# Attention of a post-norm transformer layer: normalised in 32x32 blocks turned by VectorE, with new orders of all steps

## What is computed

```python
qkv = x @ Wqkv + bqkv                      # 16 heads of 16
scores = q @ k.T / 4 + alibi_causal_bias   # per head, -inf above the diagonal
out = softmax(scores) @ v                  # per head
x = layernorm(x + out @ Wo + bo)
wu, wg, wd = ternary_quant(W_up), ternary_quant(W_gate), ternary_quant(W_down)
x = layernorm(x + (silu(x @ wu.T) * (x @ wg.T)) @ wd.T)
```

## Time and profile before

| | |
|---|---|
| time, median of 3 runs | 621.96 us (621.37 to 624.52) |
| span of the profiled execution | 619.3 us (its own time is not listed beside the span) |
| PE busy | 583.6 us (94%) |
| DVE busy | 494.4 us (80%) |
| ACT busy | 318.8 us (51%) |
| POOL busy | 299.0 us (48%) |
| DMA | 68.49 MB, mean 111 GB/s |
| chain that ended last | PE 78%, DVE 5%, ACT 5%, POOL 5%, issue 4%, DMA 2% |

### The profile page before, as it was taken

How to read it: one execution, slowest core, us unless ns; L and a number is a source line. 1 busy time by engine, 2 the same in 40 slices (tenths; PEclk the granted TensorE clock), 3 DMA queues, 4 the chain that set the end, 5 groups by cost and what they waited for, 6 DMA issues and landing times.

```text
span 619.3 us, 12888 instructions
## 1 busy us (share of the span) xinstructions
PE 583.6 (94%) x4012; PEld 342.5 (55%) x4012; DVE 494.4 (80%) x1258; ACT 318.8 (51%) x593; POOL 299.0 (48%) x504
## 2 busy tenths in 40 slices
PE   5789888999999999999999999999999999999995
PEld 3344354664656555674556646575556646446674
DVE  5388968996799868989599877989599877993766
ACT  2129713459247644477246653476345753576262
POOL 1306695346275535465174543654264452654234
PEclk9789998999999999999999999999999999999998
DMA  6965715005462073502653064601644054600101
GB/s 158 289 175 206 211 51 161 23 29 163 122 172 66 3 229 115 166 1 83 161 166 100 1 199 123 160 28 52 186 144 127 1 166 105 206 2 3 35 1 35
DMA packets 47724, 68.49 MB, mean 111 GB/s; under 512 B 4857, under 2 KB 43641, under 8 KB 44793
## 3 DMA queue, kind: packets, MB, share of 16 engines
q1 hardware_dynamic: 47691, 68.08, 37.5%
HBM read 38.44 MB, written 29.36 MB: 109 GB/s over the span
## 4 chain that ended last, share of the span: by engine, by line
PE 78%; DVE 5%; ACT 5%; POOL 5%; issue 4%; DMA 2%; SPq 0%; POOLq 0%; DVEq 0%
PE ring L698 17%; PE max_bank L613 10%; PE acc L647 9%; PE ring L635 9%; PE ring L590 8%; PE acc L715 7%; PE ring L597 4%; ACT probs L772 4%; PE ring L671 4%; PE max_bank L618 2%; PE ring L655 2%; POOL probs L1042 2%; PE ring L684 1%; POOL tern_down L1085 1%; PE max_bank L715 1%
## 5 line engine op out<-in xcount | busy, mean ns | idle before, releaser
L772 ACT ACTIVATE probs<-ring 128x512 f32<-128x512 f32 x320 | 170.7, 606 | 45.6 <-PE ring L635 44.0
L1042 POOL TENSOR_SCALAR_AFFINE_SELECT probs<-probs 128x256 f32<-128x256 f32 (+1 forms) x320 | 120.5, 401 | 130.1 <-ACT probs L772 129.4
L896 DVE CUSTOM_DVE_ANT_0 max_bank<-max_bank,causal_wide 128x384 f32<-128x384 f32 (+1 forms) x256 | 157.2, 637 | 15.3 <-PE max_bank L613 12.2
L613 PE MATMUL max_bank<-k_stack,q_stack 112*128 112x384 bf16 (+3 forms) x512 | 123.4, 304 | 5.9 <-DVE neg_max L896 2.8
L1078 POOL TENSOR_TENSOR hidden_lo<-hidden,hidden_hi 128x512 f16<-128x512 f32 (+1 forms) x72 | 75.1, 1050 | 63.6 <-ACT hidden_hi L803 63.3
L635 PE MATMUL ring<-q_stack,k_stack 114*128 114x512 bf16 (+3 forms) x512 | 103.7, 300 | 1.6 <-DVE attn L921 0.5
L791 ACT ACTIVATE gating<-ring,tanh_scale 128x512 f32<-128x512 f32 (+1 forms) x72 | 45.8, 639 | 74.0 <-PE ring L698 74.0
L647 PE MATMUL acc<-probs,v_ones 128*32 128x512 f32 (+3 forms) x1024 | 79.9, 437 | 2.8 <-POOL probs L1042 2.8
L613 PEld LDWEIGHTS max_bank<-k_stack,q_stack 112*128 112x128 bf16 x512 | 46.5, 98 | 54.0 <-DVE neg_max L896 15.3
L900 DVE TENSOR_REDUCE neg_max<-max_bank 128x2 f32<-128x512 f32 (+1 forms) x96 | 63.7, 686 | 10.4 <-PE max_bank L618 8.7
L635 PEld LDWEIGHTS ring<-q_stack,k_stack 114*128 114x128 bf16 x512 | 44.5, 97 | 49.4 <-issue 17.0
(11 more groups left out here) (107 smaller groups left out, 866.0 us busy)
## 6 DMA issues: line engine op xcount, KB each, us to landing
q_stack<-qk_scratch SPq DMA_DIRECT2D x15, 768.0 KB, 6.1
k_stack<-k_slots SPq DMA_DIRECT2D x15, 768.0 KB, 7.8
qk_scratch<-qk_parts SPq DMA_DIRECT2D x16, 384.0 KB, 3.0
k_slots<-qk_parts SPq DMA_DIRECT2D x16, 384.0 KB, 2.6
xin<-x_dram SPq DMA_DIRECT2D x8, 512.0 KB, 3.5
qk_scratch<-qk_parts SPq DMA_DIRECT2D x16, 256.0 KB, 3.2
k_slots<-qk_parts SPq DMA_DIRECT2D x16, 256.0 KB, 2.3
res<-x_dram SPq DMA_DIRECT2D x8, 512.0 KB, 3.4
```

The source lines that it names most:

```text
L613: mm = pe.matmul(max_bank[k][:, width * i:width * (i + 1)], q_stack[0:MAX_ROW, 4 * g + h, P * tile:P * (tile + 1)], k_stack[0:MAX_ROW, 4 * ...
L772: rg.drained(act.activation(probs[:, g % 2, n, :], rg.bank(step)[:, :], ACT.Exp), step)
L896: dve.tensor_tensor_reduce(scores, scores, causal_wide[:, SEQ - width:SEQ], -1.0, LOWEST_START, ALU.add, ALU.min, neg_max[:, g, first_col: ...
L1042: return pool.affine_select(out=v, in_=v, compare_op=ALU.is_ge, fill=0.0, base=0, pattern=([[0, blocks]] if blocks > 1 else []) + [[1, P]] ...
```

## The change

1. **Turns on VectorE.** A head's block in the accumulator is 32 partitions wide, so it can be turned in 32x32 blocks. The new step `turn.g` turns the whole accumulator block by block on VectorE from PSUM into `pv_t`, in place of the copy. Now queries lie in the partitions within each block, 32 columns for each group of 32 queries. `nt_out.g` takes reciprocal and product straight from `pv_t` and writes 16 columns of each block of `mixed[f]`: the even quad of the pair to the first 16, the odd to the last. `at.f` turns `mixed[f]` back in blocks on VectorE into `attn_t`. The steps `nt` and `at` are gone from TensorE, the two copies from ScalarE and VectorE, and both from the ring.
2. **Wo's rows.** As features now come out in another order (pairs of heads, 32 partitions), Wo is loaded a second time with its rows permuted, by eight transfers (`load_wo.1`); the plain Wo for folding the bias is loaded into `attn_t`.
3. **V in pairs.** `v.u` computes two tiles of tokens into one bank, and one ScalarE instruction reads them out: two of each a batch in place of four.
4. **Orders.** All lists but PRE are written anew. PRE only gets `load_wo.0` for `load_wo`.

The diff of the code, cut to its core:

```diff
         inv_sum = sb("inv_sum", [P, 2, TT * 4, 1], F32)
-        attn = sb("attn", [P, TT, HID], F32)
+        mixed = sb("mixed", [P, FT, SEQ], F32)
...
                     elif kind == "load_wo":
-                        sp.dma_start(bias_o[:, :], b_o.unsqueeze(0).broadcast_to([P, HID])).then_inc(weights_in[1], 16)
-                        sp.dma_start(wo[:, :, :], w_o.rearrange("(t p) n -> p t n", p=P)).then_inc(weights_in[1], 16)
+                        if step[1] == 0:
+                            sp.dma_start(bias_o[:, :], b_o.unsqueeze(0).broadcast_to([P, HID])).then_inc(weights_in[1], 16)
+                            sp.dma_start(attn_t[:, :, 0:HID], w_o.rearrange("(t p) n -> p t n", p=P)).then_inc(weights_in[1], 16)
+                        else:
+                            rows = w_o.rearrange("(f e h d) n -> f h e d n", f=FT, e=2, d=DH)
+                            for f in range(FT):
+                                for h in range(4):
+                                    sp.dma_start(wo[32 * h:32 * (h + 1), f, :], rows[f, h]).then_inc(wo_in, 16)
...
                     elif kind == "v":
-                        t = step[1]
-                        if first and t == 0:
+                        u = step[1]
+                        if first and u == 0:
...
                         for f in range(FT):
-                            mm = pe.matmul(bank[:, 0:HID], x_t[:, f, P * t:P * (t + 1)], wqkv[:, f, 2 * HID:3 * HID],
-                                           start=(f == 0), stop=(f == FT - 1))
+                            for i in range(2):
+                                mm = pe.matmul(bank[:, HID * i:HID * (i + 1)], x_t[:, f, P * (2 * u + i):P * (2 * u + i + 1)],
+                                               wqkv[:, f, 2 * HID:3 * HID], start=(f == 0 and i == 0), stop=(f == FT - 1),
+                                               skip_group_check=True)
...
                             if g == 0:
-                                rg.wait_drained(pe, ("v", TT - 1))
+                                rg.wait_drained(pe, ("v", TT // 2 - 1))
...
                             mm.then_inc(acc_filled[g % 2], 1)
-                    elif kind == "nt":
-                        g = step[1]
-                        at_least(pe, acc_drained[g % 2], 3, b, g // 2 + 1 - acc_skipped(name))
-                        for t in range(TT):
-                            mm = pe.transpose(bank[:, P * t:P * (t + 1)], pv_t[:, g % 2, P * t:P * (t + 1)], ident[:, :])
-                        rg.filled(mm, step)
-                    elif kind == "at":
-                        f = step[1]
-                        rg.wait_all_drained(pe, (("nt", 2 + f),), step)
-                        for t in range(TT):
-                            mm = pe.transpose(bank[:, P * t:P * (t + 1)], attn[:, t, P * f:P * (f + 1)], ident[:, :])
-                        rg.filled(mm, step)
...
                         if u == 0:
-                            rg.wait_drained(pe, ("at", f))
-                            pe.wait_ge(weights_in[1], 32)
+                            at_least(pe, attn_turned, FT, b, f + 1)
+                            pe.wait_ge(wo_in, 16 * 4 * FT)
...
                         for f in range(FT):
-                            mm = pe.matmul(bank[:, 0:HID], bias_rows[:, f, :], wo[:, f, :], start=(f == 0), stop=(f == FT - 1))
+                            mm = pe.matmul(bank[:, 0:HID], bias_rows[:, f, :], attn_t[:, f, 0:HID], start=(f == 0), stop=(f == FT - 1))
...
                     elif kind == "v_out":
-                        t, v = step[1], ("v", step[1])
-                        if first and t == 0:
+                        u, v = step[1], ("v", step[1])
+                        if first and u == 0:
...
                         rg.wait_filled(act, v)
-                        rg.drained(act.activation(v_ones[:, t, :, 0:DH], rg.bank(v)[:, 0:HID].rearrange("p (h d) -> p h d", d=DH),
-                                                  ACT.Copy), v)
+                        rg.drained(act.activation(
+                            v_ones[:, 2 * u:2 * u + 2, :, 0:DH].rearrange("p t h d -> p (t h) d"),
+                            rg.bank(v)[:, :].rearrange("p (c d) -> p c d", d=DH), ACT.Copy), v)
...
                         rg.drained(act.activation(probs[:, g % 2, n, :], rg.bank(step)[:, :], ACT.Exp), step)
-                    elif kind == "pv" and step[1] < 2 and step[2] == TT - 1:
-                        g = step[1]
-                        at_least(act, acc_filled[g % 2], 3, b, g // 2 + 1 - acc_skipped(name))
-                        act.activation(pv_t[:, g % 2, :], acc[g % 2][:, :], ACT.Copy).then_inc(acc_drained[g % 2], 1)
-                    elif kind == "at":
-                        rg.wait_filled(act, step)
-                        rg.drained(act.activation(attn_t[:, step[1], :], rg.bank(step)[:, :], ACT.Copy), step)
...
                         dve.tensor_tensor(lo, qk_rest[:, t, :], mid, ALU.subtract).then_inc(qk_split[0], 1)
-                    elif kind == "pv" and step[1] >= 2 and step[2] == TT - 1:
+                    elif kind == "turn":
                         g = step[1]
+                        if not (first and g == 0):
+                            at_least(dve, mixed_done, QUADS, b, g - 1)
                         at_least(dve, acc_filled[g % 2], 3, b, g // 2 + 1 - acc_skipped(name))
-                        dve.tensor_copy(pv_t[:, g % 2, :], acc[g % 2][:, :]).then_inc(acc_drained[g % 2], 1)
+                        dve.transpose(pv_t[:, g % 2, :], acc[g % 2][:, :]).then_inc(acc_drained[g % 2], 1)
...
                         g = step[1]
-                        nt = ("nt", g)
-                        rg.wait_filled(dve, nt)
-                        heads = rg.bank(nt)[:, :].rearrange("p (s c) -> p s c", c=32)
+                        heads = pv_t[:, g % 2, :].rearrange("p (s c) -> p s c", c=32)
+                        at_least(dve, acc_drained[g % 2], 3, b, g // 2 + 1 - acc_skipped(name))
...
                         at_least(dve, inverted, QUADS, b, g + 1)
-                        rg.drained(dve.tensor_tensor(
-                            attn[:, :, 4 * DH * g:4 * DH * (g + 1)].rearrange("p t (h d) -> p t h d", d=DH),
-                            heads[:, :, 0:DH].rearrange("p (t h) d -> p t h d", t=TT),
-                            inv_sum[:, g % 2, :, :].rearrange("p (t h) o -> p t h o", t=TT).broadcast_to([P, TT, 4, DH]),
-                            ALU.mult), nt)
+                        dve.tensor_tensor(
+                            mixed[:, g // 2, :].rearrange("p (s c) -> p s c", c=32)[:, :, DH * (g % 2):DH * (g % 2 + 1)],
+                            heads[:, :, 0:DH], inv_sum[:, g % 2, :, :].broadcast_to([P, TT * 4, DH]),
+                            ALU.mult).then_inc(mixed_done, 1)
+                    elif kind == "at":
+                        f = step[1]
+                        at_least(dve, mixed_done, QUADS, b, 2 * f + 2)
+                        dve.transpose(attn_t[:, f, :], mixed[:, f, :]).then_inc(attn_turned, 1)
...
                         if u == 0:
-                            if name == "SEVENTH":
-                                dve.wait_ge(y_done, TT * b)
+                            if not first:
+                                at_least(dve, y_done, TT, b, 0)
...
```

More of the change, by code:

```diff
@@ L165 @@
+    turn.3 pv.3.2 pv.3.3 wo.0.0 nt_out.3 wo.1.0 at.1 wo.0.1 wo.1.1 store stack_read.0
 """
 LOOP_ORDER = """
[L168 to L171 removed]
@@ L205 @@
[L205 to L209 removed]
+    v.0 v_out.0 take.0.0 part_write.3.0 take.0.1 max.0.0 max.0.1 ln1 qk.2 take.0.2 split.2 max.0.2 x1t.0 max.0.3
```

179 lines of the change are left out of this document (90 added, 89 removed).

## The result

| | before | after |
|---|---|---|
| median | 621.79 us (621.37 to 624.52, 4 runs) | 631.30 us (628.85 to 632.72, 4 runs) |
| span of the profiled execution | 619.3 us | 627.0 us |
| ratio after/before | | 1.0154 (95%: 1.0113 to 1.0195) |

A forecast was written before the change was run, and what follows sets the result against it. TensorE, busy 70.02 of 70.70 us in a LOOP iteration, was taken as the bound. Five iterations -12.2, FIRST and SECOND -3, SEVENTH and LAST -2.4 gave -17.6 us: forecast 604.5 us, range 593 to 615.

The forecast's parts named there:

- What bounds the kernel: In LOOP, TensorE's queue of matmuls sets the end; what leaves TensorE comes off the period until another chain is late.
- What leaves TensorE (-3.6): At the end of an iteration, the nt and at transposes and their waits leave TensorE: 3.6 us an iteration.
- The turn (0.69) and VectorE (+2.8): A turn on VectorE takes 0.69 us; VectorE's load grows by 2.8 us an iteration, to 62.4 us.
- wo.0.1's wait (0.6): At an iteration's end, wo.0.1 waits 0.6 us (0.3 to 1.2) for VectorE's last turn, reciprocal, product and at.1.
- The layer norm and the stack (0.55; bounds 0.2 to 2): At a LOOP iteration's start, TensorE waits for x1t.0's chain or k_stack's landing, together 0.55 us.
- The junction (-3; range -8 to +3): FIRST and SECOND together get 3 us shorter, from an earlier GpSimd chain, fewer transposes, less filler and a new wait.
- about 1.5 us sooner: In FIRST, GpSimd's masks end about 1.5 us sooner (-1 to 4), as TensorE and ScalarE lose work.
- SEVENTH and LAST (-2.4): nt.0, nt.1 and the shorter way to z save 2.4 us; LAST's new order costs nothing (-1 to +1).
- Rival 1: Queue gives part back: wait for stack or x1t.0 2 us an iteration, or junction +3; 612 us; chance 0.17.
- Rival 4: The new orders undo the saving by more waits of max units for takes; 622 us, no change; chance 0.05.
- Rival 2: VectorE becomes the bound if a turn takes 1.38 us, deciding from 1.1 us; 635 us; chance 0.05.
- the port rule: GpSimd and a two-port or two-input VectorE instruction lock each other out; an at turn might hold a mask 0.69 us.

The follow-up runs named there:

- experiments 5: Kernel after with qk.1 moved sooner and turn.1, nt_out.1 moved behind split.1 in LOOP; 634.2 us, ratio 1.0212.
- 12: Kernel after with SP's output store in LOOP held until k_stack has landed; 630.4 us, ratio 1.0158.
- 8: Kernel after with two unused turns of 0.69 us added on VectorE ahead of mt_out.0 in LOOP; 636.3 us, ratio 1.022.
- 9: Kernel after with one wait added in LOOP: GpSimd begins split.2 only after VectorE's four normalisations; 622.9 us, ratio 1.0025.
- 10: Kernel before with load_res moved behind split.3 in LOOP, so that split.2 runs beside the normalisations; 627.8 us, ratio 1.0108.
- pool_waits: Kernel after with GpSimd's split.2 in LOOP waiting for VectorE's four normalisations, the same run as 9; 622.9 us, ratio 1.0025.
- Experiment 3: Kernel after with FIRST and SECOND alone in the lists of the kernel before; 627.4 us, ratio 1.0073.
- Experiment 14: In the kernel before and in best, ternary.2.2 moved from FIRST to behind split.3 in SECOND; 617.3 us (0.9949) and 615.1 us (0.9915).
- best: Kernel after with GpSimd's wait for the normalisations, the store after k_stack's landing, and FIRST and SECOND lists of the kernel before; 620.4 us, 0.9993.
- experiment 1: Kernel after with FIRST, SECOND, LOOP, SEVENTH and LAST in the lists of the kernel before, turn.g in place of nt.g; 633.5 us, ratio 1.0177.
- v0_first: Kernel after with v.0 moved ahead of x1t.0 in LOOP; 626.1 us, ratio 1.0064.
- store_later: Kernel after with the output store in LOOP held until k_stack has landed, the same run as 12; 630.4 us, ratio 1.0158.
- dve_extra: Kernel after with two unused VectorE turns added in LOOP, the same run as 8; 636.3 us, ratio 1.022.
- load_res_first: Kernel after with load_res moved ahead of split.2 in LOOP, as in the kernel before; 635.0 us, ratio 1.0206.

## Why the prediction was wrong, step by step

- **What bounds the kernel.** TensorE at 70.02 of 70.70 us was right as a row, and wrong as a rule for what comes next: the chains beside it had about no slack. When experiments 5 and 12 took away the wait at max.0.0, the period did not fall, as x1t.0 waited instead; when 8 gave VectorE more work, it grew; when 9 took away the collision, it fell.
- **What leaves TensorE (-3.6).** qk.1 to wo.0.0 became 11.31 - 8.62 = 2.7 us shorter where 2.6 was forecast, though 0.2 to 0.3 of it is exp.3.3, which now stands ahead of qk.1 (an estimate from the 0.22 to 0.33 us between the starts of such units). TensorE's busy time fell by only 2.1; the time is lost again between qk.2 and qk.1 (below).
- **The turn (0.69) and VectorE (+2.8).** 0.71: right. VectorE's row grew by 4.5, not 2.8: the turns brought 2.9 (4 x 0.712 + 2 x 0.706 - 2 x 0.692), the slowed normalisations 1.5.
- **wo.0.1's wait (0.6).** 0.48: right.
- **The layer norm and the stack (0.55; bounds 0.2 to 2).** *This step failed.* It counted the chain z, rstd, normalisation with the old durations, and looked only at TensorE's filler. That GpSimd's list had changed from `ln1 load_res split.2` to `ln1 split.2 split.3 load_res`, so that split.2 runs beside the normalisations, I had in the lists and did not price. The trace of the kernel before showed the price once, at the start of SECOND, where split.2 follows rstd too and x1t's second half waited 1.22 us:

```profile
94.94 3.42 DVE L820 TENSOR_SCALAR x<-z,mean_var,rstd 128x256 f32<-128x256 f32 x4 [0.43 <-POOL rstd L1073]
```

Experiment 9 takes it away (-1.41 us an iteration, -8.4 us in all), 10 makes it in the old kernel (+1.1%). k_stack's wait was 1.00 us where I had it within half a microsecond. Its issue came 0.7 us sooner after qk.1, as forecast (7.35 us, against 8.06). The landing took 0.9 us longer, by the store that I had counted as a gain for standing behind the read.
- **What still lacks.** Without the collision the period is 69.57, where 68.2 was forecast. Of the 1.37 us that are left, 0.68 at max.0.0 is near what the sum had for that place (0.55). The rest lies between qk.2 and qk.1: 56.66 us in pool_waits against 55.22 before. Less the wait of 0.68, and with nt.0 gone (0.49) and exp.3.3 come in, that is about 1 us that TensorE's row doesn't show as idle. Its weight loads' row has the nine waits for takes shown above, 2.4 us against 0.6, in pool_waits as in the kernel after. That these make the 1 us is my reading; experiment 8, where more work of VectorE's made the waits for takes and the period grow, speaks for it. The term that failed here is VectorE's load, 62.7 of 69.57 us, which I had at zero.
- **The junction (-3; range -8 to +3).** It came to +6.8 us. *This step failed too, by 9.8 us.* The masks end at 83.97 instead of 76.84; the last five take 5.03 us beside VectorE's ternary instructions, against 4.65 in the earlier trace rows, so that term was about right ("no difference"). What was wrong is "about 1.5 us sooner": they came 7.1 us later. The granted clock over the first 91.8 us is 0.83, against 0.93 over the first 91.5 before; TensorE waited 1.87 us for q_stack's row maxima and 5.29 us for masks. Behind the masks FIRST lost 2.9 us more, a wait for its last at turn, which the sum had only for SECOND (+0.6). And rstd no longer waited for GpSimd, as the forecast had it, but for VectorE:

```profile
94.20 1.99 PE L670 MATMUL ring<-wo_w,attn_t 128*128 128x256 f32 x8 [2.89 <-DVE attn_t L922]
```

```profile
99.44 1.04 POOL L1070 TENSOR_TENSOR rstd<-var_eps,half_neg 128x4 f32<-128x4 f32 x1 [0.42 <-DVE var_eps L828]
```

So SECOND begins 10.0 us later (96.03, against 86.05) and wins 3.2 back. Experiment 3 gives back some 4 to 5 us with the old lists. Experiment 14 is no part of this loss: its edit gains 0.5% in the kernel before too (0.8% in best). Which of the moved steps in FIRST made the masks late is open: the one that I tested, load_wo.1, gave no clear answer.
- **SEVENTH and LAST (-2.4).** -0.7. x1t.0 of LAST starts 6.8 us later than before (595.24, against 588.47), where 8.4 had come up to the LOOP's end: SEVENTH gained 1.6. LAST lost 0.9, counted at nothing: after TensorE's waits of 1.35 and 0.96 us at the end of SEVENTH, the granted clock was 0.51 from 597.9 to 601.4, where it was 1.00 in the same part of the kernel before.
- **The rivals.** Rival 1 had the place (wait for the stack or x1t.0, 2 us an iteration) but not the cause. Rival 4, at 0.05, was nearest: new orders that undo it. It named more waits of max units for their takes, and the weight loads show them, beside the collision, which it did not name. Rival 2's condition, a turn above 1.1 us, did not hold; its mechanism, VectorE's load, shows in experiment 8 at two thirds of the price. I had quoted the port rule in the prediction and used it only for the masks.

## What to carry to other kernels

When an order changes, list for every engine which pairs of instructions now run at the same time, not only what each waits for. Here VectorE's normalisations, and in experiment 1 a product of two SBUF inputs, took about two and seven times as long beside GpSimd, while the turns did not slow; a short instruction of VectorE's on the path to TensorE is the one that pays. A wait can be the cheaper order: holding GpSimd back for 1.9 us brought 1.3%. And an engine that is busy 99% says what an iteration with this work can't go below, not that removed work comes back as time; the next chain must be counted with its new neighbours.

## What the runs showed that I had not expected

- A VectorE instruction of 128x4 elements took 3.09 us instead of 0.17 beside one of GpSimd's of 4.07, while turns from PSUM and from SBUF kept to 0.70 and 0.71 beside the same chain.
- The start varies between executions of the same lists. FIRST is the same in ten of the kernels, among them after, v0_first, pool_waits, store_later and dve_extra. In these five SP issues its last read of k_stack at 75.19, 72.85, 74.41, 74.89 and 81.14 us, with a granted clock over the first 70 us of 0.85, 0.90, 0.85, 0.85 and 0.80. In these five a later read goes with a lower clock, though not in all ten: load_res_first issues it at 75.37 with 0.90. So a difference of 2 to 3 us in the median of few runs can come from there, and the period in LOOP is the better measure.
